# A two-layer transformer kernel on one core: attention outputs normalised by way of DRAM, a third chain of stages, and a new rule for the written-out order

## The reference

```python
x = x + L0_attn(layernorm(x))    # 16 heads of 16, causal softmax, v, output matrix
x = x + L0_ffn(layernorm(x))     # entmax15 gate of 16 experts; 256->128, gate; 128->1024, gelu; 1024->128, gate; 128->256
x = x + L1_attn(layernorm(x))    # folded low-rank q, k, v; rotary on half of each head; causal softmax
x = x + L1_ffn(layernorm(x))     # shared expert 256->128->256 with squared relu; routed experts only if trunc(prob) is not 0
```

## Time and profile before

| what | us |
|---|---|
| median of 3 runs | 2942.04 (2939.97 to 2944.25) |
| the profiled execution's own time | 2941.76 |
| its span, first to last instruction | 2940.0 |
| PE busy | 2637.8 (90%) |
| DVE busy | 2091.0 (71%) |
| ACT busy | 1895.6 (64%) |
| POOL busy | 948.8 (32%) |

### The profile page before, as it was taken

One profiled execution on the slowest core, in us unless ns is written; L12 is line 12 of the kernel. 1 busy time (PEld: TensorE's weight loads), 2 busy tenths in 40 slices (PEclk: granted clock), 3 DMA queues, 4 the chain that ended last, 5 costly groups with the idle time before them and its releaser, 6 DMA issues.

```text
span 2940.0 us, 56496 instructions
## 1 busy us (share of the span) xinstructions
PE 2637.8 (90%) x18768; PEld 1101.7 (37%) x18853; DVE 2091.0 (71%) x5808; ACT 1895.6 (64%) x3868; POOL 948.8 (32%) x1646
## 2 busy tenths in 40 slices
PE   6989998999889998999989999899988999889987
PEld 4334432334333443334433343333433334333432
DVE  4865687857868588685887668776687757878483
ACT  3565665767566766667666675576766776566655
POOL 2214241425214251243413234142521425114411
PEclk9999999999999999999999999999999999999999
DMA  5202120212102120121211112011210213101120
GB/s 185 55 1 60 44 55 18 68 47 80 37 27 64 57 80 18 32 75 45 75 26 42 56 58 69 19 58 42 77 49 24 62 46 89 31 25 46 32 59 16
DMA packets 138734, 150.43 MB, mean 51 GB/s; under 512 B 15920, under 2 KB 122832, under 8 KB 138448
## 3 DMA queue, kind: packets, MB, share of 16 engines
q1 hardware_dynamic: 138448, 146.74, 17.3%
HBM read 78.46 MB, written 67.11 MB: 50 GB/s over the span
## 4 chain that ended last, share of the span: by engine, by line
PE 64%; ACT 13%; DVE 13%; issue 5%; POOL 1%; DMA 1%; SPq 0%; ACTq 0%; DVEq 0%; POOLq 0%
PE ps L1254 15%; PE ps L1170 9%; ACT probs L1557 9%; PE ps L1235 7%; PE ps L1194 7%; PE ps L1162 6%; DVE mx L1824 4%; PE ps L1333 4%; PE ps L1328 4%; DVE ps L1821 4%; PE ps L1119 2%; PE ps L1320 2%; PE ps L1262 2%; PE ps L1208 1%; PE ps L1137 1%
## 5 line engine op out<-in xcount | busy, mean ns | idle before, releaser
L1557 ACT ACTIVATE probs<-ps 128x512 f32<-128x512 f32 (+2 forms) x2560 | 1235.0, 564 | 371.5 <-PE ps L1235 365.5
L1824 DVE TENSOR_REDUCE mx<-ps 128x1 f32<-128x512 f32 (+2 forms) x1536 | 900.3, 639 | 251.5 <-PE ps L1208 125.9
L1821 DVE CUSTOM_DVE_ANT_0 ps<-ps,mask_b 128x512 f32<-128x512 f32 (+1 forms) x1024 | 614.6, 650 | 251.4 <-PE ps L1194 249.6
L1729 POOL TENSOR_SCALAR_AFFINE_SELECT probs<-probs 128x256 f32<-128x256 f32 (+1 forms) x768 | 368.8, 484 | 1110.9 <-ACT probs L1557 1108.5
L1254 PE MATMUL ps<-probs,vaug 128*17 128x512 f32 (+3 forms) x6144 | 618.7, 513 | 8.7 <-ACT probs L1557 3.7
L1194 PE MATMUL ps<-stk_k,stk_q 48*128 48x512 f16 (+3 forms) x3072 | 458.3, 333 | 60.8 <-issue 36.6
L1235 PE MATMUL ps<-stk_q,stk_k 50*128 50x512 f16 (+3 forms) x3072 | 439.0, 333 | 63.5 <-ACT probs L1557 20.5
L1194 PEld LDWEIGHTS ps<-stk_k,stk_q 48*128 48x128 f16 x3072 | 138.1, 94 | 437.8 <-issue 347.3
L1235 PEld LDWEIGHTS ps<-stk_q,stk_k 50*128 50x128 f16 x3072 | 131.5, 94 | 440.8 <-issue 338.4
L1162 PE MATMUL ps<-turned,wqkv 128*128 128x512 f32 x512 | 262.0, 619 | 9.2 <-ACT scratch L1522 2.1
L1254 PEld LDWEIGHTS ps<-probs,vaug 128*17 128x17 f32 x6144 | 139.6, 98 | 295.9 <-issue 202.0
(11 more groups left out here) (171 smaller groups left out, 2902.0 us busy)
## 6 DMA issues: line engine op xcount, KB each, us to landing
stk_q<-q SPq DMA_DIRECT2D x256, 96.0 KB, 2.5
stk_k<-k SPq DMA_DIRECT2D x128, 192.0 KB, 3.6
q<-parts SPq DMA_DIRECT2D x64, 256.0 KB, 2.3
k<-parts SPq DMA_DIRECT2D x64, 256.0 KB, 2.2
stk_k<-k SPq DMA_DIRECT2D x128, 96.0 KB, 2.5
x<-in_L_attn_x SPq DMA_DIRECT2D x16, 512.0 KB, 4.0
q<-parts SPq DMA_DIRECT2D x64, 128.0 KB, 2.8
k<-parts SPq DMA_DIRECT2D x64, 128.0 KB, 2.1
```

What stands on the lines that cost most here:

```text
L1557: act.activation(probs[:, step % PBUF, heads, cols], src, ACT.Exp, scale=exponent[l])\
L1729: pool.affine_select(out=diag, in_=diag, compare_op=ALU.is_ge, fill=0.0, base=0, pattern=[[0, k], [1, P]], channel_multiplier=-1).then_inc ...
L1821: dve.tensor_tensor_reduce(tile, tile, mask_b[:, BANK - width:BANK], 1.0, LOWEST, ALU.add, ALU.max, most)\
L1824: dve.tensor_reduce(most, tile.rearrange("q (k w) -> q k w", k=k), AX.X, ALU.max)\
```

## The change

1. **Outputs through DRAM.** `nm` and `yt` go, with `y`, `rec` and their transposes. Instead SP stores `oT` of every unit to DRAM (`os`). For every second unit, SP loads two units' 16 output rows a head as 128 partitions of `yT` and their sums as a 128 x 32 tile (`ol`). DVE inverts the sums (`rc`), SP stores the inverses (`rs`), loads them spread over the 16 rows of each head (`rl`), and POOL multiplies (`dv`). `yT` has one buffer; `ao` reads it.
2. **Three chains.** Layer 1's `attended` and `second_ffn` move to a third chain. `turned` gets a third slot. The feed-forward part has its own tiles (`ffn`) with eight Gelu buffers, so all `hid` come first and hold "gelu", and the eight `z` follow without it.
3. **Order.** `mx` gets four slots. Two new ranks pull `s` forward when DVE, and `st` when ACT, is about to run out of work by the planner's count. The constants change.
4. **No constant products.** `keep_going` and `FILL` go.
5. **Smaller.** The cosine product is made in place behind the shuffle (`qc` goes), squared relu is in place (`hq` goes), and `parts` has three buffers in place of four.

```diff
-PRING = 4
+MXN = 4
+PRING = 3
+SLOT_OF = (1, 0, 1, 2)
-LEAD = 9.0
-PACE = 0.9
-DENSE = 2.0
-SPREAD = 1.0
+LEAD = 8.39
+PACE = 0.82
+DENSE = 1.74
+SPREAD = 0.93
...
+def divided(u):
+    b, l, g, c = UNITS[u]
+    k = PASSES.index((b, l, c))
+    if g % 2 == 0:
+        return []
+    steps = [("after", ("os", u))]
+    if k >= YT and g == 1:
+        steps.append(("after", ("ao", *PASSES[k - YT], TPC // 2 - 1)))
+    return steps + [([(kind, u)], "") for kind in ("ol", "rc", "rs", "rl", "dv")]
...
-    for o in range(OC + 1):
-        steps += [([("hid", b, c, o)], "+gelu" if o == 0 else "")] if o < OC else []
-        steps += [([("z", b, c, o - 1)], "-gelu" if o == OC else "")] if o else []
+    steps += [([("hid", b, c, o)], "+gelu" if o == 0 else "-gelu" if o == OC - 1 else "") for o in range(OC)]
+    steps += [([("z", b, c, o)], "") for o in range(OC)]
...
-            out.append(([(b, 0, 1)], attended(b, 0, 0) + attended(b - 1, 1, 0) + first_ffn(b, 0) + second_ffn(b - 1, 0), []))
+            out.append(([(b, 0, 1)], attended(b, 0, 0) + first_ffn(b, 0), [], attended(b - 1, 1, 0) + second_ffn(b - 1, 0)))
...
-            choices.append((time, RANK['late'] if late(plan.s_unit, len(plan.s_items)) > 0 else RANK['s'], plan.score, ()))
+            choices.append((time, RANK['late'] if late(plan.s_unit, len(plan.s_items)) > 0 else RANK['fed'] if plan.busy['DVE'] - now < FEED_DVE else RANK['s'], plan.score, ()))
...
-                choices.append((time, RANK['st'], "st", main[0]))
+                choices.append((time, RANK['fed_st'] if plan.busy['ACT'] - now < FEED_ACT else RANK['st'], "st", main[0]))
...
-STAY = 2.1
-RANK = dict(mt=1, nm=2, burst=3, late=4, st=5, pair=5.5, due=6, s=7, chain=8, single=10)
+STAY = 2.1
+FEED_DVE = 2.0
+FEED_ACT = 0.6
+FED = 2
+FED_ST = 3.4
+ST = 7.19
+S = 6.96
+LATE = 4.0
+DUE = 7.04
+PAIR = 5.16
+CHAIN = 8.0
...
+            def store_o(u):
+                sp.wait_ge(o_drained, u + 1)
+                sp.dma_start(o_d[u], oT[:, u % 2]).then_inc(o_stored[u % 2], 16)
+
+            def load_o(u):
+                b, l, g, c = UNITS[u]
+                k, kd = PASS[b, l, c], g // 2
+                for v in (u - 1, u):
+                    sp.wait_ge(o_stored[v % 2], 16 * (v // 2 + 1))
+                if k >= YT and kd == 0:
+                    written(sp, ("ao", *PASSES[k - YT], TPC // 2 - 1))
+                if DIVIDED["dv", u]:
+                    sp.wait_ge(y_ready, DIVIDED["dv", u])
+                strips = o_d[u - 1:u + 1].rearrange("u (h s) n -> (u h) s n", s=STRIP)
+                sp.dma_start(yT[:, k % YT, kd], strips[:, 0:DH]).then_inc(o_loaded, 16)
+                sp.dma_start(sums[:], strips[:, DH].rearrange("h (a n) -> h a n", n=STRIP)).then_inc(o_loaded, 16)
+
+            def store_inverse(u):
+                sp.wait_ge(inverted, DIVIDED["dv", u] + 1)
+                sp.dma_start(inverse_d[u], sums[:]).then_inc(inverse_stored, 16)
+
+            def load_inverse(u):
+                sp.wait_ge(inverse_stored, 16 * (DIVIDED["dv", u] + 1))
+                heads = inverse_d[u].rearrange("(h d a) n -> h d (a n)", h=MH, d=1)
+                sp.dma_start(inverse[:], heads.broadcast_to([MH, DH, BANK])).then_inc(inverse_loaded, 16)
...
-            def keep_going(key, pt):
-                if FILL.get(key, 0) and key == next(iter(FILL)):
-                    pe.wait_ge(pool_chain, 9)
-                for _ in range(FILL.get(key, 0)):
-                    pe.matmul(pt, ident_b[:], mask_b[:], start=True, stop=True)
...
-            def normalise(u):
-                out, done = claim(("nm", u))
-                pe.wait_ge(o_drained, u + 1)
-                for i in range(TPC):
-                    ins = pe.transpose(out[:, P * i:P * (i + 1)], oT[:, u % 2, P * i:P * (i + 1)], ident[:])
-                ins.then_inc(done, 1)
...
+            def divide(u):
+                b, l, g, c = UNITS[u]
+                y = yT[:, PASS[b, l, c] % YT, g // 2]
+                pool.wait_ge(o_loaded, 32 * (DIVIDED["dv", u] + 1))
+                pool.wait_ge(inverse_loaded, 16 * (DIVIDED["dv", u] + 1))
+                pool.tensor_tensor(y, y, inverse[:], ALU.mult).then_inc(y_ready, 1)
...
+            def invert(u):
+                dve.wait_ge(o_loaded, 32 * (DIVIDED["dv", u] + 1))
+                dve.reciprocal(sums[:], sums[:]).then_inc(inverted, 1)
```

More of the change, by code:

```diff
@@ L364, in give @@
                 self.waiting.append((item[1], time + MARGIN))
+            if item[0] == "os":
+                time = self.transfer(time, 1, 1.5)
+            if item[0] == "ol":
+                time = self.transfer(time, 2, 1.6)
+            if item[0] == "rs":
+                time = self.transfer(time, 1, 0.1)
+            if item[0] == "rl":
+                time = self.transfer(time, 1, 1.5)
             if item[0] == "p2":
@@ L422, in score @@
         if not self.s_items:
-            self.chains[4] += [("after", item)] + ([("after", ("mt", u - 1))] if u else []) + [([("most", u)], "")] * UNITS[u][3] + [([("mx", u)], "")]
+            self.chains[MAXIMA] += [("after", item)] + ([("after", ("mt", u - 1))] if u else []) + [([("most", u)], "")] * UNITS[u][3] + [([("mx", u)], "")]
             self.s_unit += 1
@@ L504, in weigh @@
             self.put(("o", u), self.out[u])
-            self.outputs.append((u, self.out[u]))
-    def may_normalise(self, u):
-        b, l, g, c = UNITS[u]
-        k = PASSES.index((b, l, c))
-        return g > 0 or k < 2 or ("yt", *PASSES[k - 2], KD - 1) in self.at
-    def normalise(self):
-        u, ready = self.outputs.pop(0)
-        self.run("nm", max(ready, self.ring_time()), 0.44)
-        end = self.on("DVE", self.pe + HOP, 0.75)
-        self.free[self.take(("nm", u))] = end
-        self.ring.append(end)
-        self.put(("nm", u), end)
 def later(step):
     item = step[0][0] if step[0] else ("",)
-    return 0.0 if item[0] in ("xt", "yt") and item[-1] else LATER.get(item[0], 0.0)
+    return 0.0 if item[0] == "xt" and item[-1] else LATER.get(item[0], 0.0)
 def takes_time(step):
@@ L561, in program_order @@
     position, gap = 0, 0.0
-    while main or todo or any(plan.chains) or plan.held or plan.outputs:
+    while main or todo or any(plan.chains) or plan.held:
         begin = todo and (not main or position >= window_end)
-        for n in range(2):
+        for n in range(MAINS):
             if todo and (begin or EARLY and not plan.chains[n]):
@@ L582, in program_order @@
             moved = False
-            for n in range(5):
+            for n in range(OUTPUTS + 1):
                 step = plan.head(n)
@@ L624, in program_order @@
                 continue
-            assert not main and not any(plan.chains) and not plan.held and not plan.outputs, (main[:1], [c[:1] for c in plan.chains], plan.locks)
+            assert not main and not any(plan.chains) and not plan.held, (main[:1], [c[:1] for c in plan.chains], plan.locks)
             continue
@@ L651, in program_order @@
         if what != "wait":
-            item = plan.order[made]
-            if gap > FILL_FROM and item[0] in ("xt", "yt", "at", "st", "mt", "s", "nm", "lg", "rt"):
-                FILL[item] = int(gap / FILL_TIME)
             gap = 0.0
@@ L673, in choice_mode @@
         kind = "mt"
-    elif what == plan.normalise:
-        kind = "nm"
     else:
@@ L681 @@
 STAY = 2.1
-RANK = dict(mt=1, nm=2, burst=3, late=4, st=5, pair=5.5, due=6, s=7, chain=8, single=10)
+FEED_DVE = 2.0
[8 more added lines that the diff above has]
+CHAIN = 8.0
+RANK = dict(fed=FED, fed_st=FED_ST,mt=1, burst=3, late=LATE, st=ST, pair=PAIR, due=DUE, s=S, chain=CHAIN, single=10)
 EARLY = True
-FILL_TIME, FILL_FROM = 0.25, 0.7
-FILL = {}
 PLACE = {}
@@ L746, in plan_transposed @@
         kind = item[0]
-        if kind in ("xt", "yt") and item[4] == 0:
+        if kind == "xt" and item[4] == 0:
             key = item[:4]
@@ L1636, in _ @@
                 elif kind == "at":
-                    done = len([1 for it in ORDER[:ORDER.index(item)] if it[0] == "p2"])
-                    act.wait_ge(parts_ready, done)
                     pt = arrived(act, item)
```

226 lines of the change are left out of this document (99 added, 127 removed).

## The result

The changed kernel takes 2829.93 us (median of 4 runs, 2825.09 to 2842.77), beside 2941.01 us for the kernel before on the same chip. The ratio is 0.9629, with a 95% interval of 0.9611 to 0.9647. It is faster by 109 us by this ratio and by 111 us by the two medians, where the sum had 163 and gave 2779 us. 2830 is inside the range given (2690 to 2885) and inside the forecast's own (2725 to 2850), but it lies nearly on the time that the rival "the clock" gives (2833).

What follows compares the result with a forecast made beforehand. PE was taken to set the pace. From 2941.76 us: transposes -76, DVE and ACT work -14, constant products -40, way through DRAM +23, order -56, giving 2779 us (ratio 0.945); range 2690 to 2885, the forecast's own 2725 to 2850.

Steps and rivals of the forecast that it cites:

- the clock: Rival: without constant products, two more half-clock stretches of 6.8 us in each of eight periods cost 54 us: 2833 us; chance 0.09.
- What bounds the kernel: PE, busy for 90% of the span and 64% of the chain; a microsecond taken from it comes off nearly whole.
- constant products: Steady part: 283 products cost PE 63 us, mostly ahead of score items; two thirds taken as gain, -40 us, bounds 0 and -63.
- order: Whole steady part: new order evens out the engines' load, a quarter of PE's 222 us idle time, -56 us.
- Transposes: `nm` and `yt` on PE: 192 groups, 84 us of work, at 91% a gain of 76 us, bounds 54 to 118.
- The reading of the one `st` at 1171.6 us: Three constant products ran after ACT freed the bank, ahead of `st`; read as costing some 0.6 us on ACT's path.
- The way through DRAM: Last output's latency 11.6 us in place of 4.0, 7.6 more, at three places where attention waits: +23 us.
- SP's queue: 384 more DMAs, about 154 us of SP's issue time, fit into its waiting time; costed at nothing.
- SP's queue blocks: Rival: SP's in-order waits delay `st` by 3 us in each of 64 groups, 192 us: 2971 us; chance 0.11.
- PE busy near 2400: Sign in the profile after that the removed work was priced right: 2638 - 118 - 119 = 2400 us.
- well fed: Rival: all steady constant products were on the path, order gives half the idle time: 2701 us, PE idle some 300; chance 0.17.
- the condition for being wrong: The prediction is wrong if PE's idle time in the steady part is outside some 220 to 400 us.

Runs made afterwards that it cites:

- experiment 5: The kernel before without constant products and with one transpose in place of four in each `nm` and `yt`, same written list: 2966.75 us, ratio 1.0085.
- experiment 1: The kernel before with every constant product left out and nothing else altered: 2950.02 us, ratio 1.0026.
- experiment 4: The changed kernel with the old ranks and constants, both feeding rules off, two chains and the old Gelu burst with `z` inside: 2964.36 us, ratio 1.008.
- experiment 3: The changed kernel with the old ranks and constants and both feeding rules off; three chains and the short Gelu burst stay: 2927.24 us, ratio 0.995.
- experiment 2: The changed kernel with 498 constant products put back where its planner waits for over 0.7 us: 2850.08 us, ratio 0.9694.
- experiment 8: The changed kernel with outputs stored to DRAM but never loaded back, inverted or multiplied; the output product reads zeros: 2808.29 us, ratio 0.9547.
- experiment 7: The changed kernel with constant products only in five long waits of PE: 2828.6 us, ratio 0.9619.

## Why the prediction was right or wrong

**What bounds the kernel.** "A microsecond taken from PE should therefore come off the span nearly whole" is the step that failed. At an equal clock about a third came off (experiment 5), and the clock, which the sum left out, fell and took that back. The windows of four periods show it, in the order before, experiments 1, 5, 4 and 3, after:

```profile
1100.00:2506.20 1406.20, 1284.45 (x9234) 535.24 (x9268) 1038.67 (x2881) 942.06 (x1928) 471.06 (x816) 0.98 0.18 51
```

```profile
1097.90:2502.30 1404.40, 1271.06 (x9106) 526.32 (x9104) 1034.16 (x2880) 941.16 (x1929) 470.78 (x816) 0.96 0.17 51
```

```profile
1096.10:2513.40 1417.30, 1272.06 (x8818) 512.43 (x8816) 1037.88 (x2880) 942.20 (x1928) 472.26 (x816) 0.94 0.17 50
```

```profile
1086.20:2508.40 1422.20, 1253.87 (x8738) 492.00 (x8736) 1005.25 (x2796) 926.91 (x1899) 520.13 (x858) 0.94 0.24 75
```

```profile
1099.30:2485.00 1385.70, 1231.65 (x8722) 497.84 (x8720) 989.40 (x2787) 930.97 (x1900) 512.20 (x852) 0.94 0.25 76
```

```profile
1057.10:2385.20 1328.10, 1220.39 (x8721) 474.40 (x8722) 1015.87 (x2785) 939.37 (x1897) 512.25 (x848) 0.97 0.26 80
```

(The first trace lacks 34 matmul records here, so its busy time reads a few us low.) Four periods take 1406.2 us before, 1404.4 without the products, 1417.3 with most transposes gone too, and 1422.2 by the way through DRAM. PE's instructions fall from 9106 to 8738 between experiments 1 and 4 and its busy time by 17 us, but its idle time (length less busy) rises from 133 to 168 us. Then the same instructions in another order take 1385.7 (chains and burst) and 1328.1 us (ranks), with 154 and 108 us idle. Time followed the order and not the amount of PE's work.

The waits of PE show what stood behind the idle time. Total us, number and longest one of experiment 1, of experiment 5, of experiment 4, and after:

```profile
PE ps L1194 <- DVE mx L1821: 15.7, 22, 2.4
PE ps L1235 <- DVE mx L1821: 15.5, 27, 0.9
...
PE ps L1235 <- DVE mx L1824: 15.2, 36, 1.2
...
PE ps L1194 <- DVE mx L1824: 5.5, 19, 0.8
```

```profile
PE ps L1194 <- DVE mx L1825: 22.8, 31, 2.4
PE ps L1235 <- DVE mx L1825: 20.7, 38, 1.3
...
PE ps L1235 <- DVE mx L1828: 17.3, 41, 1.6
...
PE ps L1194 <- DVE mx L1828: 6.1, 17, 0.9
```

```profile
PE ps L1240 <- DVE mx L1835: 41.0, 54, 3.7
...
PE ps L1240 <- DVE mx L1838: 33.9, 68, 1.8
...
PE ps L1279 <- DVE mx L1838: 23.6, 40, 1.6
...
PE ps L1279 <- DVE mx L1835: 18.8, 42, 0.8
```

```profile
PE ps L1278 <- ACT probs L1573: 67.4, 117, 1.5
...
PE ps L1278 <- DVE mx L1837: 18.9, 35, 1.8
PE ps L1278 <- DVE mx L1834: 17.1, 27, 2.2
...
PE ps L1239 <- DVE mx L1834: 11.3, 42, 0.8
PE ps L1239 <- DVE mx L1837: 10.6, 32, 2.3
```

PE's waits for DVE to take the score maxima add up to 52 us in experiment 1, to 67 in experiment 5, to 117 in experiment 4 and to 58 after. Experiments 1 and 5 have the same written list: where PE had less to do, it came sooner to the next product whose bank DVE still held. The new order hands DVE its work in time, and this wait shrinks again. It is not the whole of the gain: between experiment 4 and after it is 59 us of 134, and PE's waits for ACT's exponentials did not shrink (the lines of `s`, `st` and `pv` together: 56 us in experiment 1, 80 in experiment 4, 89 after). The profile before had this: in one window DVE was full and PE at 7.55. The prediction saw it and priced it at 56 us, and still priced the removed work as if PE set the pace.

**Term by term.** The steps from before over experiments 1 and 4 to after add up to the whole change:

| term | forecast | measured |
| --- | --- | --- |
| transposes, DVE, ACT and POOL work, way through DRAM | -76 - 14 + 23 = -67 | +14 (experiments 1 to 4) |
| constant products | -40 | +9 in the old order, -20 in the new (experiments 1, 2) |
| order: chains, burst, ranks | -56 (0 to -111) | -134 (experiment 4 to after) |
| sum | -163 | +9 + 14 - 134 = -111 |

Each measured step contains what the clock did in it. The first two terms promised 130 us too much and the third 78 too little; that these errors nearly cancel is luck. The table takes one path from before to after. Along another path the same parts have other prices, as the two figures for the products and the third chain (37 and 74 us) show.

- *Transposes.* Forecast -76, bounds -54 to -118. Experiment 5 has +17 for three quarters of them, of which the removal itself is a gain of some 10 to 20 and the clock a loss of some 30 to 40 (estimates, see experiment 5). The lower bound, 64% from PE's share of the chain of waits, excluded what happened. That chain shows what came last, not how closely DVE or ACT stood behind it, so its share is no lower bound.
- *Constant products.* The price depends on the order. In the old one they cost nothing in the steady part: over four periods their removal took 13 us from PE's busy time and added 12 us to its idle time (windows above), and the 9 us that they were worth lie in the last stretch, where they kept the clock up (experiment 1). In the new one they stand in the way. The reading of the one `st` at 1171.6 us was the wrong sample for the old order.
- *The way through DRAM.* +23 was the forecast for what it takes more than the old way, three times 7.6. Measured are 22 us for all of the way back (experiment 8), which by the same reckoning should have been 33; that 22 is near 23 is chance. Against the kernel before, the tail is 15 us longer (47.6 and 32.4 us from the last `oT` copy to the end), in place of 7.6. The latency itself is 9.4 longer (13.4 less 4.0), most of all since the loads of the sums and of the inverses took 3.9 and 3.6 us from issue to use where 2.5 was taken, and the half clock behind the wait cost 3 us on the output product at once. The other places cost less than was put down for them: of the 26 us between the profiled executions after and of experiment 8, 15 lie in the tail and 7 in the first 610 us.
- *SP's queue.* Nothing, as forecast. SP waits long, but for work that isn't there yet, such as `mT` (634.9 us, where it was 1495) and the reciprocals (158.0 us in 38 waits, the longest 7.1), and PE waited for the loads of the maxima for 1.7 us in three waits, where it was 2.6 in four. Leaving out the waits for the reciprocals and inverses altogether takes 3.5 us from four periods (experiment 8), 0.1 us for each of their 32 groups, where the rival had 3. "SP's queue blocks" is excluded. One wait for a transfer did grow, which the prediction did not name: PE's for the k stacks (`stk_k`), from 5.5 us before and 14.3 in experiment 1 to 34.7 after, the longest 12.2. It is 38.0 in experiment 8, so the way back is not its cause; what is was not tested.
- *Order.* This is the term mis-sized by most: 134 us against 56, above the upper bound of 111 that half of PE's idle time had set. That bound counted idle time alone, and only that of the kernel before. From experiment 4 to after, the spans fell by 128 us: 87 of them are idle time of PE (427 to 340), of which 78 had come with the removed work, and 41 are busy time (2533.5 to 2492.1) at the same 17565 instructions, with a mean granted clock of 0.943 in place of 0.928. The four slots of `mx` have no part in it: the planner writes the same list with two.
- *The clock.* The sum has no term for it, and that is the second step that failed. The mean clock fell from 0.975 to 0.943; as time at half clock this is 2 x 0.025 x 2940 = 147 us before and 2 x 0.057 x 2832.6 = 323 us after. What that costs can be read from executions of one and the same kernel, whose instructions and order don't differ. The four of the changed kernel go from 2823.1 us at a clock of 0.948 to 2840.8 at 0.938, the ten of experiment 1 from 2935.4 at 0.953 to 2952.4 at 0.944: both 0.3 us for each further us at half clock. The 176 us more are then some 50 us of the changed kernel's time. This is an estimate. A stretch of idle time makes an execution longer and can lower its clock too, and two other readings give 0.1 (experiment 7: 52 us less, the profiled span 6 us shorter) and 0.4 (the second stretch of experiment 5: 61 us more by the trace's clock records, 14 us of time and some 10 that the 252 transposes should have given), so 20 to 70 us. The rival's 54 lies in it. So the rival's mechanism is real, while its time, 2833 us, was met because the other errors nearly cancel. Experiment 2 does not speak against it: at 0.3 the higher clock (0.973) gives some 50 us back, and the products take some 70. The Trainium skill, "TensorE: Matmul & The Clock Gate", Part 1, has the throttled clock as the default that activity releases; the tails of experiment 7 and of the changed kernel agree with it (3.72 against 6.71 us).

Of the marks that the prediction set: PE busy near 2400 was wrong (2492), because less work at a lower clock doesn't shorten busy time in proportion. Experiment 2 shows the reverse: its 498 further products, of which the trace has 429, are 109 us at some 0.22 us each (12.26 / 56 in experiment 7), or 94 us for the 429, but PE is busy for only 40 us more (2492.1 to 2531.8). PE idle is 340, between the forecast's 379 and the 300 of well fed. The steady part's idle time, 208 us, fell outside the 220 to 400 that the prediction named as the condition for being wrong, and rightly: the order term was wrong. ACT's wait for the Gelu products fell as forecast. The clock fell below 0.96, which "would speak for the clock", and it does: what the fall costs is estimated above.

## What to carry to other kernels

Where several engines are busy for 65 to 90% and each in turn is full, work removed from the fullest one can be worth little or nothing (here a third of it at an equal clock, and less than nothing with what the clock did); price it from the waits of that engine in windows, not from its busy share or its share of the chain, and look at the granted clock of the same stretch in both kernels. A rule in the planner that pulls work forward for the engine about to run dry is the cheapest thing to try first: with its constants it gave two thirds of the whole gain here (74 of 109 us). No run shows that removing the transposes pays in any order: with two chains the kernel that keeps them was faster under the old ranks and, with its constant products, under the rules. A parallel chain is worth more once such a rule can use it (37 against 74 us), so such changes have to be tried together, and a padding product tuned under one order has to be tried again under the next.

## What the runs showed of the hardware

- Removing TensorE work can lower its granted clock and keep its busy time up. With 252 transposes fewer in 1230 us the clock went from 0.96 to 0.93 and the busy time from 1109.3 to 1112.2 us; in a stretch where the clock stayed at 0.95, 96 fewer took 9.5 us from it (experiments 1 and 5).
- Executions of one kernel differ in their mean granted clock, and their time goes with it: 0.938 to 0.948 and 2840.8 to 2823.1 us in the changed kernel, 0.944 to 0.953 and 2952.4 to 2935.4 us in experiment 1.
- 56 products of constants in the 14 us wait ahead of 16 float32 matmuls brought those from 6.71 to 3.72 us, with the granted clock at 0.54 and at 1.00 (after, and experiment 7).
- A round trip of store, load, reciprocal, store and load took 12.0 us from the end of the copy to the start of the product on POOL, with 3.9 and 3.6 us for the loads of the sums and of the inverses, although the stack loads of 96 KB took 2.5 from issue to landing.
